# Two relative attentions: the embedded values of eight score tiles, and a batch's values and folds, in every fourth step of the loop

## The chip, the core and the metric

The kernel runs on one core of a Trainium2 chip. The metric is device time in microseconds (us) of one execution of the whole program; three runs of the kernel before gave a median of 2755.65 us. The core's engines work in parallel, each through its own list of instructions in order, and meet only at semaphores: TensorE (PE; its weight loads are shown apart as PEld), VectorE (DVE), ScalarE (ACT), GpSimd (POOL), and SyncE (SP), which issues transfers here.

## What is computed

The network is a chain of residual stages on four lanes (the batch entries `c`) of 512 tokens and 128 channels. Two of its stages are attentions with relative positions, 16 heads of 8 channels. The change touches these two alone. Cut to what matters, the first is

```python
rk, rv = embk[rel], embv[rel]                       # rel = max(t - s, 0)
att = einsum('bhtd,bhsd->bhts', q, k) * scale + einsum('bhtd,tsd->bhts', q, rk)
att = softmax(where(causal, att, -inf))
y = einsum('bhts,bhsd->bhtd', att, v) + einsum('bhts,tsd->bhtd', att, rv)
```

and the second is the same with no causal mask, a distance clipped on both sides, and biases. Each output row is a sum over the keys of the values `v` (called values below) and of the embedded distances `rv` (called embedded values), both weighed by the softmax.

## The kernel before

The program is one list of stages; a `core` stage holds the loop of a relative attention. `which` is 0 for the first attention and 1 for the second. A score tile `t` is 8 queries x 16 heads = 128 rows against all keys in reach; there are 256 of them per attention (`TILES`), `t.G` is their number, and 16 tiles make a batch (`BATCH`), so there are 16 batches. With `which` 0 a batch reaches 1, 2, 3 or 4 blocks of 128 keys (`t.nk`), by turns; with `which` 1 always 4.

The loop is the same on every engine: `core_steps` yields `T_` = 0, 2, 4, ..., and each piece of work is done for the tiles that lag behind `T_` by a constant. One step treats two tiles. On PE a step is:

- `scores` of tiles `T_`-6 and `T_`-5 into banks 0 and 1, each after the exponential of the tile two before has freed the bank (`r_exp`); its last two matmuls (the near positions) also wait for `r_diagonal`;
- `spread` in every second step (`T_` % 4 == 0): the queries of four tiles repeated into bank 6, from which DVE makes the operand `B4` (`diagonal`);
- `turn`: the weights of tiles `T_`-8 and `T_`-7 transposed into banks 2 and 3;
- `inverse` once in a batch;
- in every second step (`T_` % `QUAD` == 0, the step that has a `spread`) what I call a **burst**: `embedded` of four tiles (narrow matmuls of 32 output columns into bank 4 or 5), and in two of a batch's four bursts four of the eight parts of `values` and one `fold` (two matmul groups, also 32 columns wide, into bank 7, or bank 6 with `which` 1). `values` of a batch needs all 16 tiles turned and copied; `fold` needs the embedded values of eight tiles, picked out by DVE's `chosen`.

A step with neither spread nor burst is called plain, and two steps, a plain one and one with a spread, make a pair; a batch has four pairs.

ACT does, in a step, `exps` of two tiles (L1400, each with a read of its sum) and `turned`, the copies of two turned tiles (L1307) into `PT`. `PT` has three slots of eight tiles, so the first copy of every second slot waits for `r_values`, the end of the values of the batch that used the slot before. DVE does, in a step and in this order, `chosen` (L1749, one of four tiles), `position_copy` (L1783 and L1788, only `which` 1, after a fold), `head_copy` (L1809 and L1810, after a batch's values), `inverse` (L1735 and L1737), `maxima` of two tiles (L1765) and `diagonal` (L1758). POOL spreads the queries (L1960, L1970) some steps ahead.

The constants are lags: `EMBED` for `embedded`, `CHOSEN` for `chosen`, `FOLDS` for the two folds of a batch (one pair per attention), `VALUES` for the first part of `values`, `INVERSE`, and `VALUES + QG` for `head_copy`.

## Time and profile before

| | |
|---|---|
| median of three runs | 2755.65 us (2753.82, 2755.65, 2778.35) |
| the profiled execution: its time, its span | 2761.87 us, 2759.9 us |
| PE busy | 2608.3 us (95%) |
| ACT busy | 1839.9 us (67%) |
| DVE busy | 1640.8 us (59%) |
| POOL busy | 1028.1 us (37%) |
| first loop (`which` 0) | from about 612 us to about 1000 us |
| second loop (`which` 1) | from about 1130 us to about 1672 us |

In the timeline a row is a run of like instructions: start, length, engine, line, operation, output<-inputs, shape, count, and in brackets what ended an idle time before it. Every matmul of PE stands on helper lines (L807, L1052), so the work is told by its operands: `table_keys,halves` begins `scores`, `halves,exact` is `spread`, L1052 with `const,low` or `const,slot` is `turn`, `low,table_low` (or `low,shifted`) with 32 columns is `embedded`, `low` alone with 32 columns is `values`, and `slot,const` with 32 columns is `fold`. One matmul of a narrow group is two records. Since matmuls are pipelined, a piece of work is best measured from its first start to the first start of what follows it.

### The profile page before, as it was taken

How to read it: one execution, taken by the hardware profiler on the slowest of the kernel's cores; microseconds unless marked ns; L12 is line 12 of the kernel's file. 1: busy time of each engine (PE TensorE's matmuls, PEld its weight loads, DVE VectorE, ACT ScalarE, POOL GpSimd, SP SyncE). 2: the span in 40 equal slices, each digit the busy share in tenths (PEclk: the TensorE clock that was granted, in tenths of full speed). 3: DMA queues.
4: the chain of work that ended last, by engine and by line, in shares of the span. 5: the costliest groups of instructions: out<-in, count | busy, mean ns of one | idle time of the engine just before them, and what ended most of it. 6: DMA issues, size and time to landing. Idle time of an engine off the chain costs nothing.

```text
span 2759.9 us, 61490 instructions
## 1 busy us (share of the span) xinstructions
PE 2608.3 (95%) x23878; PEld 1795.5 (65%) x23878; DVE 1640.8 (59%) x4295; ACT 1839.9 (67%) x4424; POOL 1028.1 (37%) x876
## 2 busy tenths in 40 slices
PE   7999999999999999999999998998998998988998
PEld 4655656559889884688888884554455664553554
DVE  6564747475455447656665666774774336755774
ACT  6676767526676671778787876875886417766775
POOL 2323324213333320545454543552553015543551
PEclk9999999999999999999999999999999999999999
DMA  1010000000000001000000003210210002101110
GB/s 59 1 44 1 14 4 7 4 9 2 3 2 2 2 2 57 25 2 2 2 2 2 2 2 126 49 36 20 62 44 8 24 14 68 47 20 37 48 39 16
DMA packets 35411, 63.13 MB, mean 23 GB/s; under 512 B 11542, under 2 KB 15670, under 8 KB 34102
## 3 DMA queue, kind: packets, MB, share of 16 engines
q1 hardware_dynamic: 35126, 59.21, 7.8%
q8 instruction: 194, 3.18, 0.5%
q14 instruction: 91, 0.75, 0.1%
HBM read 23.62 MB, written 1.15 MB: 9 GB/s over the span
## 4 chain that ended last, share of the span: by engine, by line
PE 76%; DVE 8%; ACT 8%; issue 3%; SPq 3%; POOL 1%; DMA 1%; DVEq 0%; POOLq 0%; ACTq 0%
PE bank L807 65%; PE bank L1052 6%; PE bank L1189 3%; SPq L772 3%; ACT work L1339 1%; ACT work L1446 1%; PE bank L893 1%; ACT squared L1317 1%; ACT bank L1315 1%; DVE work L1635 1%; ACT squared L1311 1%; DMA work<-work 1%; DVE centered L1566 1%; POOL work L2009 1%; ACT work L1307 1%
## 5 line engine op out<-in xcount | busy, mean ns | idle before, releaser
L1765 DVE TENSOR_REDUCE low<-bank 128x1 f32<-128x512 f32 (+22 forms) x512 | 292.9, 573 | 294.5 <-PE bank L807 292.9
L1307 ACT ACTIVATE low<-bank 128x512 f32<-128x512 f32 (+3 forms) x544 | 434.4, 920 | 0.9 <-PE bank L1052 0.9
L807 PE MATMUL bank<-table_keys,halves 128*128 128x512 f32 (+3 forms) x1536 | 416.5, 379 | 2.6 <-ACT low L1400 2.5
L807 PEld LDWEIGHTS bank<-work 128*64 128x64 f32 (+4 forms) x4192 | 248.4, 144 | 203.0 <-issue 150.1
L807 PE MATMUL bank<-work 128*64 128x128 f32 (+6 forms) x4192 | 343.1, 294 | 38.9 <-DVE work L1859 20.4
L1400 ACT ACTIVATE low<-bank,low 128x512 f32<-128x512 f32 (+23 forms) x384 | 225.0, 586 | 231.3 <-DVE low L1765 226.0
L1960 POOL TENSOR_TENSOR halves<-squared,const 128x512 fp32r<-128x512 f32 x128 | 135.7, 1060 | 507.3 <-PE bank L807 507.3
L1307 ACT ACTIVATE work<-bank 128x512 f32<-128x512 f32 (+4 forms) x389 | 199.2, 538 | 130.5 <-PE bank L807 68.3
L807 PEld LDWEIGHTS bank<-table_keys,halves 128*128 128x128 f32 x1536 | 243.5, 190 | 42.2 <-issue 11.9
L1446 ACT ACTIVATE work<-work 128x192 f32<-128x192 f32 (+1 forms) x512 | 218.7, 431 | 38.4 <-DVE work L1852 38.4
L2009 POOL TENSOR_TENSOR work<-work 128x768 f32<-128x768 f32 x128 | 187.7, 1467 | 138.4 <-DVE work L1863 138.4
L2014 POOL TENSOR_TENSOR work<-work 128x512 f32<-128x512 f32 x128 | 163.4, 1277 | 173.6 <-DMA work<-work 154.2
L807 PE MATMUL bank<-normed,slot 128*128 128x512 f32 x440 | 200.0, 597 | 6.1 <-ACT work L1358 2.4
L807 PEld LDWEIGHTS bank<-halves 128*128 128x128 f32 x1024 | 183.7, 190 | 29.1 <-DVE halves L1758 1.2
L807 PE MATMUL bank<-halves 128*128 128x128 f32 (+27 forms) x1024 | 201.9, 279 | 0.6 <-DVE halves L1758 0.5
L1311 ACT ACTIVATE squared<-centered 128x512 f32<-128x512 f32 x80 | 50.0, 629 | 223.3 <-DVE centered L1566 223.0
L807 PE MATMUL bank<-work,slot 128*128 128x512 f32 (+1 forms) x408 | 192.3, 608 | 5.6 <-ACT work L1307 5.6
L1052 PE MATMUL bank<-const,low 128*128 128x128 f32 x1248 | 182.0, 275 | 2.3 <-ACT low L1307 2.1
L1920 POOL TENSOR_SCALAR normed<-normed,slot 128x512 f32<-128x512 f32 x48 | 75.4, 1571 | 285.8 <-DVE normed L1573 285.5
L807 PE MATMUL bank<-centered,const 128*128 128x512 f32 x256 | 145.4, 650 | 27.9 <-ACT centered L1423 27.9
L2003 POOL TENSOR_TENSOR work<-work 128x512 f32<-128x512 f32 (+1 forms) x64 | 107.5, 1680 | 147.9 <-DVE work L1649 146.7
L1052 PEld LDWEIGHTS bank<-const,low 128*128 128x128 f32 x1248 | 145.0, 141 | 23.1 <-issue 3.2
(203 smaller groups left out, 5385.9 us busy)
## 6 DMA issues: line engine op xcount, KB each, us to landing
work<-work SPq DMA_DIRECT2D x512, 64.0 KB, 2.0
slot<-in_wW SPq DMA_DIRECT2D x4, 1605.5 KB, 6.6
slot<-in_wA SPq DMA_DIRECT2D x4, 837.0 KB, 6.0
table_low<-embv_padded SPq DMA_DIRECT2D x2, 1536.0 KB, 6.3
table<-in_dft SPq DMA_DIRECT2D x1, 3072.0 KB, 11.7
slot<-in_wE SPq DMA_DIRECT2D x2, 584.0 KB, 3.7
squared<-in_x SPq DMA_DIRECT2D x4, 256.0 KB, 5.9
shifted<-embv_padded SPq DMA_DIRECT2D x2, 512.0 KB, 8.3
```

The source lines that it names most:

```text
L772: sp.dma_start(R2[to:to + step, s.n % 3, :], RS[a:a + step, s.n % 3, :]).then_inc(sem(f"w_swapped{s.n % 3}"), 16)
L807: return pe.matmul(o, l, r, start=start, stop=stop)
L1052: last = pe.transpose(o[:, b * P:(b + 1) * P], PR[t.G % 4][:, b * P:(b + 1) * P], ident)
L1189: last = pe.transpose(o[:, (2 * a + blk) * P:(2 * a + blk + 1) * P], PW[:, s.n % 3, 2 * u + a, blk * P:(blk + 1) * P], ident)
L1307: return act.activation(dst, src, ACT.Identity)
L1400: act.activation(PR[t.G % 4][:, 0:n], bank[t.G % 2][:, 0:n], ACT.Exp, bias=NBR[:, t.G % 4:t.G % 4 + 1], accum_out=RSR[:, t.batch % 2, t.g: ...
L1446: last = act.activation(row, row, ACT.Exp, scale=-1.0, bias=small[:, one:one + 1], accum_out=small[:, 4 + one:5 + one])
L1765: dve.tensor_reduce(out=NBR[:, t.G % 4:t.G % 4 + 1], in_=bank[t.G % 2][:, 0:score_columns(t)], axis=AX.X, op=ALU.max, negate=True).then_in ...
L1960: pool.tensor_tensor(A4[:, half, Q % 2, :].rearrange("p (t h) -> p t h", h=HEADS_R), bc(one_lane.unsqueeze(2), [P, 4 * QG, HEADS_R]), bc(k ...
L2003: pool.tensor_tensor(row, row, bc(small_a[:, 8 + s.i % 4, 0:LOC].unsqueeze(2), [P, LOC, 256 - lo]), ALU.mult)\
L2009: pool.tensor_tensor(row, row, bc(small_w[:, s.n % 4, 8:12].unsqueeze(2), [P, 4, 192]), ALU.mult).then_inc(sem("w_weighed"), 1)
L2014: pool.tensor_tensor(R1[:, s.n % 3, :], R1[:, s.n % 3, :], R2[:, s.n % 3, :], ALU.add).then_inc(sem("w_added"), 1)
```

## The change

`embedded` is done for eight tiles at a time, in every fourth step (`T_` % 8 == 0) instead of for four in every second step. All eight parts of a batch's `values` are done in one burst, eight steps of `T_` later than they began before, with the folds after the first part. With `which` 0 both folds of a batch go there; with `which` 1 the first fold goes to the other burst of the batch and the second here. `chosen` and `head_copy` lag accordingly, and the loop has one more step at its end. So a batch has two bursts instead of four, a small one (eight embedded tiles, with `which` 1 one fold) and a big one (eight embedded tiles, the folds, all values). The number of matmuls, activations and vector instructions of the loops stays.

```diff
-SCORES, TURN, EMBED, CHOSEN, QUAD = 6, 8, 12, 14, 4
-FOLDS, VALUES, INVERSE = ((24, 28), (24, 28)), 24, 22
-STEPS = TILES + BATCH + 2
+SCORES, TURN, EMBED, CHOSEN, QUAD, BURST = 6, 8, 16, 18, 4, 8
+FOLDS, VALUES, INVERSE, HEADS = ((32, 32), (24, 32)), 32, 22, 34
+STEPS = TILES + BATCH + 4
...
-                    if T_ % QUAD == 0:
-                        for j in range(QUAD):
+                    if T_ % BURST == 0:
+                        for j in range(BURST):
                             st(embedded, EMBED - j)
                         values(T_)
-                        values(T_ + 1)
                         fold(T_)
-                        values(T_ + 2)
-                        values(T_ + 3)
+                        for j in range(1, BURST):
+                            values(T_ + j)
...
-                        dve.wait_ge(sem("r_head_copied"), BATCHES + sum(VALUES + QG + BATCH * one < T_ for one in range(BATCHES)))
+                        dve.wait_ge(sem("r_head_copied"), BATCHES + sum(HEADS + BATCH * one < T_ for one in range(BATCHES)))
...
-                    k = batch_after(T_, VALUES + QG)
+                    k = batch_after(T_, HEADS)
```

The first place is PE in the second loop, near its end. Before, two bursts of one batch, each between the transposes of a step and the scores of the next (in the order a narrow matmul counts once, so `x16` is four tiles):

```order
L1052 MATMUL bank<-const,low 128x128 x8
L807 MATMUL bank<-low,table_low 32x16x4 x16
L807 MATMUL bank<-low 32x128 x16
L807 MATMUL bank<-slot,const 32x64 x16
L807 MATMUL bank<-low 32x128 x16
L807 MATMUL bank<-table_keys,halves 128x512 x3
L807 MATMUL bank<-halves 128x192 x2
```

Now the big burst at the same place of a batch:

```order
L1052 MATMUL bank<-const,low 128x128 x8
L807 MATMUL bank<-low,table_low 32x16x4 x32
L807 MATMUL bank<-low 32x128 x8
L807 MATMUL bank<-slot,const 32x64 x16
L807 MATMUL bank<-low 32x128 x56
L807 MATMUL bank<-table_keys,halves 128x512 x3
L807 MATMUL bank<-halves 128x160 x2
```

The embedded matmuls are doubled, and 64 values matmuls stand in one place where 32 stood in each of two.

The second place is DVE in the second loop, over the part of a batch in which its position copies (L1783 and L1788 before, one line up in the changed kernel) and head copies (L1809, L1810) stand. Before:

```order
L1749 TENSOR_TENSOR slot<-bank,const 128x4x16x8
L1783 TENSOR_TENSOR low<-bank,low 32x64 x4
L1788 SCALAR_TENSOR_TENSOR centered<-low,centered 32x4x64
L1765 TENSOR_REDUCE low<-bank 128x1 x4
L1758 TENSOR_TENSOR halves<-bank,const 128x512
L1749 TENSOR_TENSOR slot<-bank,const 128x4x16x8
L1783 TENSOR_TENSOR low<-bank,low 32x64 x4
L1788 SCALAR_TENSOR_TENSOR centered<-low,centered 32x4x64
L1765 TENSOR_REDUCE low<-bank 128x1 x2
L1809 TENSOR_TENSOR low<-bank,low 128x64
L1810 TENSOR_TENSOR centered<-centered,low 128x64
```

Now, after the small burst and then after the big one:

```order
L1748 TENSOR_TENSOR slot<-bank,const 128x4x16x8
L1782 TENSOR_TENSOR low<-bank,low 32x64 x4
L1787 SCALAR_TENSOR_TENSOR centered<-low,centered 32x4x64
L1764 TENSOR_REDUCE low<-bank 128x1 x4
L1757 TENSOR_TENSOR halves<-bank,const 128x512
L1748 TENSOR_TENSOR slot<-bank,const 128x4x16x8
L1764 TENSOR_REDUCE low<-bank 128x1 x4
L1757 TENSOR_TENSOR halves<-bank,const 128x512
L1748 TENSOR_TENSOR slot<-bank,const 128x4x16x8
L1782 TENSOR_TENSOR low<-bank,low 32x64 x4
L1787 SCALAR_TENSOR_TENSOR centered<-low,centered 32x4x64
L1808 TENSOR_TENSOR low<-bank,low 128x64
```

The second position copy has moved one pair later and the head copies have come to stand right behind it, ahead of the maxima; `chosen` stands where it stood, but two of a batch's four no longer have a burst just ahead of them.

## Rows read from the trace of the kernel before

**Rows 1.** Busy time by engine, 100 us of the second loop (stretch, length, engines, clock).
```profile
1340.00:1440.00 100.00, 99.83 (x1498) 86.42 (x1498) 61.39 (x117) 81.51 (x150) 52.71 (x52) 1.00 0.01 2
```

**Rows 2.** PE's waits, second loop, 1240 to 1640 us (us in total, times, longest).
```profile
PE bank L807 <- ACT low L1400: 0.5, 3, 0.2
```

**Rows 3.** PE's timeline in the second loop: two pairs, with bursts.
```profile
1385.45 1.07 PE L1052 MATMUL bank<-const,low 128*128 128x128 f32 x8
1386.45 0.65 PE L807 MATMUL bank<-low,table_low 128*32 128x64 f32 x32
1387.04 0.96 PE L807 MATMUL bank<-table_keys,halves 128*128 128x512 f32 x3
...
1393.84 0.96 PE L807 MATMUL bank<-table_keys,halves 128*128 128x512 f32 x3
...
1400.35 0.65 PE L807 MATMUL bank<-low,table_low 128*32 128x64 f32 x32
1400.82 1.06 PE L807 MATMUL bank<-low 128*32 128x128 f32 x32
1401.69 0.63 PE L807 MATMUL bank<-slot,const 128*32 128x64 f32 x32
1402.14 1.06 PE L807 MATMUL bank<-low 128*32 128x128 f32 x32
1403.13 0.96 PE L807 MATMUL bank<-table_keys,halves 128*128 128x512 f32 x3
```

**Rows 4.** PE's timeline where the second loop starts: a pair without burst.
```profile
1133.73 0.97 PE L807 MATMUL bank<-table_keys,halves 128*128 128x512 f32 x3 [0.67 <-ACT low L1400]
...
1136.15 1.03 PE L1052 MATMUL bank<-const,low 128*128 128x128 f32 x8
1136.94 0.94 PE L807 MATMUL bank<-table_keys,halves 128*128 128x512 f32 x3
...
1139.85 0.96 PE L807 MATMUL bank<-table_keys,halves 128*128 128x512 f32 x3
```

**Rows 5.** ACT's timeline in the second loop: one step and the next exponentials.
```profile
1406.64 2.01 ACT L1307 ACTIVATE low<-bank 128x512 f32<-128x512 f32 x2
1408.44 0.64 ACT L1400 ACTIVATE low<-bank,low 128x512 f32<-128x512 f32 x1
...
1409.07 0.68 ACT L1400 ACTIVATE slot<-bank,low 128x512 f32<-128x512 f32 x1
...
1409.73 2.10 ACT L1307 ACTIVATE low<-bank 128x512 f32<-128x512 f32 x2
```

**Rows 6.** DVE's timeline in the second loop: a position copy and the next maximum.
```profile
1402.39 0.97 DVE L1783 TENSOR_TENSOR low<-bank,low 32x64 f32<-32x64 f32 x4 [0.63 <-PE bank L807]
1403.40 0.47 DVE L1788 SCALAR_TENSOR_TENSOR centered<-low,centered 32x256 f32<-32x256 f32 x1
1404.38 0.69 DVE L1765 TENSOR_REDUCE low<-bank 128x1 f32<-128x512 f32 x1 [0.51 <-PE bank L807]
```

**Rows 7.** PE's timeline in the first loop, one block of keys: scores, spread, turn.
```profile
736.97 0.51 PE L807 MATMUL bank<-table_keys,halves 128*128 128x128 f32 x3
...
737.65 0.67 PE L807 MATMUL bank<-halves,exact 128*128 128x512 f32 x2
738.16 0.38 PE L1052 MATMUL bank<-const,low 128*128 128x128 f32 x2
```

**Rows 8.** DVE's timeline in the same stretch: a maximum and the diagonal.
```profile
737.17 0.28 DVE L1765 TENSOR_REDUCE low<-bank 128x1 f32<-128x120 f32 x1 [0.77 <-PE bank L807]
...
738.36 0.69 DVE L1758 TENSOR_TENSOR halves<-bank,const 128x512 fp32r<-128x512 f32 x1 [0.22 <-PE bank L807]
```

**Rows 9.** DVE's timeline in the first loop: chosen, inverse, next maxima.
```profile
716.17 0.69 DVE L1749 TENSOR_TENSOR slot<-bank,const 128x512 f32<-128x512 f32 x1 [0.71 <-PE bank L807]
716.78 0.24 DVE L1735 RECIPROCAL low<-low 128x16 f32<-128x16 f32 x1
...
717.26 0.66 DVE L1765 TENSOR_REDUCE low<-bank 128x1 f32<-128x128 f32 x2
```

## Prediction

> **What bounds the kernel now.** I read the busy time by stretch first. In the second loop PE is busy 99.83 of 100 us at a granted clock of 1.00, which is its 2.4 GHz level, ACT 81.51 and DVE 61.39 [rows 1]. So time moves there only if PE's stream gets shorter or PE begins to wait. The view of waits says that PE waits for ACT only 0.5 us in 400 [rows 2]. That is not the whole story, because a matmul record lasts until its modelled end and hides a short wait; so I measured from first start to first start in PE's timeline. A pair of steps with a burst of embedded values alone takes 1393.84 - 1387.04 = 6.80 us; the next pair, whose burst also holds values and a fold, takes 1403.13 - 1393.84 = 9.29 us, the once-a-batch inverse included [rows 3].
>
> The row that decides the case stands at the start of the second loop, where nothing is embedded yet: a pair without a burst. It takes 1139.85 - 1133.73 = 6.12 us [rows 4]. So a burst's removal can be read directly, with what PE then waits for.
>
> **What a burst costs beyond its matmuls.** After eight transposes the first narrow matmul starts 1386.45 - 1385.45 = 1.00 us after the first transpose [rows 3]; where scores follow instead, they start 1136.94 - 1136.15 = 0.79 us after it [rows 4]. So entering costs 0.21. Four embedded tiles take 1387.04 - 1386.45 = 0.59 if scores follow, and 1400.82 - 1400.35 = 0.47 if values follow [rows 3]; so leaving costs 0.12. The Trainium skill's page "TensorEngine Tiling (Array Packing)", Tiling Modes, Key Properties, says that changing the tiling mode drains TensorE; the trace agrees with these 0.21 and 0.12, and by that rule alone each burst taken away is worth their sum.
>
> Two bursts of four go in every batch, 64 in both loops. By pure PE time that is 64 x 0.33 = 21 us. By whole pairs it is less: 6.80 less its 0.47 of embedded work is 6.33, against the 6.12 measured without a burst, so 0.21 per burst and 0.42 per batch. The difference of 0.12 is a wait that shows up when the burst no longer covers it: ACT and DVE use a burst to catch up.
>
> **Second loop, part by part, for a batch without its inverse** (which is the same in both). From the same rows, two parts of values take 1401.69 - 1400.82 = 0.87, a fold 1402.14 - 1401.69 = 0.45 [rows 3].
>
> Before: two pairs of 6.80 and two with 6.80 + 2 x 0.87 + 0.45 = 8.99, sum 31.58. After: two pairs without burst, 2 x 6.12; the small burst's pair 6.80 + 0.47 + 0.45 = 7.72; the big burst's pair 6.80 + 0.47 + 0.45 + 4 x 0.87 = 11.20; sum 31.16. That is -0.42 per batch. Three things are given back.
>
> (a) The position copy. It starts 0.25 after its fold ends (1402.39 against 1402.14) and DVE is free after 0.97 + 0.04 + 0.47, at about 1403.9, or 1.8 after the fold's end [rows 3, 6]. Today two parts of values follow the fold, and the next maximum starts 1404.38 - 1403.13 = 1.25 after its scores do, held by PE and not by the copy. After the small burst no values follow: scores start 0.12 after the fold, so the maximum could start at 1.37. It starts at 1.8, so about 0.45 late, and behind the maximum stand the exponential and, through `r_exp`, the scores of two tiles later. A plain step has no slack there. I charge it in full: +0.45 per batch. The lower bound is nothing, if the next step's spread absorbs it. After the big burst the copy lies under 3.0 us of values and costs nothing; if that cover were gone it would cost the same 0.45.
>
> (b) ACT's pace. In a step ACT needs 0.63 and 0.66 for two exponentials and 1.80 for two copies, 3.09 [rows 5], so 6.18 per pair, against 6.12 for a pair without burst. It has no idle time left in these pairs: +0.06 for each of two, +0.12 per batch. Behind the big burst the two copies that wait for `r_values` start only at its end. They take 1.80 from 0.2 after it, so until 2.0; the first exponential of the next step needs its maximum, which starts at 1.3 and takes 0.69, so it is ready at 2.0 as well. I charge nothing for it, and it is the tightest place of the change.
>
> (c) The end of the loop. The last fold now needs a `chosen` that stands behind a position copy in DVE's queue: from the end of the last embedded tiles 0.45 (fold) + 0.25 + 1.5 (copy) + 0.7 (chosen) = 2.9, where PE gets there after 0.45 + 0.43 = 0.9; it waits about 2.0, and of that 0.7 comes back, since the copy that ended the loop before is out of the way. +1.3 once.
>
> Sum of the second loop: 16 x (-0.42 + 0.45 + 0.12) + 1.3 = +3.7 us.
>
> **First loop.** The gain is the same 0.42 per batch at most. ACT has room there, having one to four blocks to treat. But DVE's queue is tight where scores are short. With one block of keys the spread starts at 737.65, the transposes at 738.16, and DVE's diagonal at 738.36 [rows 7, 8]. Without a burst the next scores start some 0.2 after the transposes do (an estimate: 0.79 is for eight), and a tile's take 737.65 - 736.97 = 0.68, so they end at 739.04 and their maximum could start 0.20 later, as 737.17 follows 736.97: at 739.24. DVE now goes from the diagonal straight to `chosen` (0.61, as the diagonal too has) and reaches the maximum at 738.36 + 0.61 + 0.61 = 739.58, 0.34 late. In the step that also has the inverse (717.26 - 716.78 = 0.48 [rows 9]) it is 0.82 late. Each further block of keys gives PE about 0.3 more (from 0.2 and 0.68 here to 0.79 and, as 1.25 less the 0.20, 1.05 with four), while DVE's queue stays: 0.04 and 0.52 with two blocks, 0 and 0.22 with three, 0 with four. Sum 1.94 over four batches, 0.49 per batch, charged in full, since the scores of these steps wait for their exponential. 16 x (-0.42 + 0.49) = +1.1 us.
>
> Together +4.8, against the profiled execution's 2761.87 us: 2766.7. That execution lies 6.2 above the median of the runs; on the median's scale it is 2755.65 + 4.8 = **2760.5 us**. What a measurement can tell from no change is about 1%, 27.6 us; every term here is below it.
>
> **Rivals.**
>
> *The gain lands whole.* If the 0.12 that ACT and DVE take back were an effect of the loop's start and (a), (b) and the first loop's queue were absorbed, it is 64 x 0.33 = 21 us faster: 2734.5. With half of the losses it is about 2748. For it: the skill's drain rule above, and PE's 99.83%. Against: the pair without burst is already 0.12 per burst slower than its matmuls. Chance of the part under 2750: 0.20.
>
> *Slower, by ACT's blocked copies.* The copies of two tiles stand in ACT's queue ahead of the next two exponentials and wait for the end of the big burst. The Trainium skill's page "TensorE: Matmul & The Clock Gate", Part 1, Engine queue depths, says that ScalarE's queue is strictly first in, first out; no run here shows an exception. By that rule nothing of the exponentials could pass, and if they had been ready all along the copies would cost their whole 1.80. The point at which it decides is 2.0 us behind the burst, where copies and maximum meet. Every 0.1 by which the copies are later costs 32 x 0.1 = 3.2 us; wholly exposed it is 16 x 1.80 in the second loop, and about two thirds of that in the first with its shorter copies: 48 us, 2804. Against the whole price: the maxima cannot be ready before the scores that follow the burst. Chance of over 2783: 0.08; of a part of it, 2768 to 2783, 0.17.
>
> *PE's clock falls.* The big burst is 0.94 + 0.45 + 3.48, nearly 5 us of narrow matmuls, where 2.78 stood (1403.13 - 1400.35) [rows 3] at full clock [rows 1]. If half of each in the second loop went at 1.2 GHz, 16 x 2.5 = 40 us: 2800. Against it: the narrow matmuls follow each other without a gap. Chance 0.03.
>
> *No effect beyond noise, as forecast*, 2750 to 2768: the remaining 0.52. Under 2728 there is no case, only the unknown; I leave it 0.03, taken from the first rival's share.
>
> **How the numbers follow.** The range reaches from 2735, where the whole gain stands, to 2781, where half of the blocked copies' price does; about 0.1 is left out above and little below. Faster by over 1%: 0.03. Slower by over 1%: 0.08 + 0.03 = 0.11, of which I give 0.10, since the lower ends of these cases stay inside. Within 1%: 0.87.
>
> **What would show it.** In the changed kernel's timeline: pairs without burst of about 6.2 us in the second loop; a big burst's pair of 11.2 and a small one's of 7.7, followed by a plain step 0.45 longer than the others, with the position copy ahead of its maximum. In the views of waits and of DVE: in the first loop with one block of keys, maxima that start right behind `chosen` with no idle time before them. ACT's idle time falls together into one place per batch, the big burst. The forecast is wrong if pairs without burst take 6.3 or more (then ACT is the bound, and it is slower), if they take under 6.05 (then it is faster), or if the clock of a stretch of 100 us falls under 1.00.

## The result, and the profile after

| | before | after |
|---|---|---|
| median | 2760.07 us (8 runs, 2753.82 to 2778.35) | 2785.22 us (8 runs, 2782.39 to 2786.23) |
| ratio after / before | | 1.0083 (95% interval 1.0068 to 1.0097) |
| the profiled execution: time, span | 2761.87, 2759.9 us | 2785.75, 2783.8 us |
| first loop, first spread to last narrow matmul | 424.8 us | 438.5 us |
| second loop, the same | 540.8 us | 556.2 us |

The change makes the kernel 25 us (0.8%) slower. The two loops lose 13.7 and 15.4 us; the stretch between them takes 93.3 us in both profiles. The stages behind the second loop take 1084.0 us where they took 1088.9; in the profiles of the experiments below the same stages take 1082.8 to 1103.1, so that difference is not put down to the change. Everything that is to be explained is in the loops. (The first loop of the kernel before ends at 1036.9 us, not at about 1000.)

The view of windows, second loop (columns as in [rows 1]):

```profile
1340.00:1440.00 100.00, 97.10 (x1502) 84.28 (x1503) 60.20 (x110) 74.96 (x143) 47.20 (x44) 1.00 0.01 2
```

PE was busy 99.83 of 100 us [rows 1] and now is 97.10, at the same granted clock of 1.00. PE has begun to wait. The view of waits of PE (us in total, times, longest), over both loops, of the kernel before (612 to 1671 us):

```profile
PE bank L1052 <- ACT low L1307: 2.7, 5, 0.9
PE bank L807 <- ACT low L1400: 2.5, 10, 0.7
PE bank L807 <- issue: 1.0, 3, 0.4
...
PE bank L807 <- DVE halves L1758: 0.5, 1, 0.5
```

and of the changed kernel (612 to 1700 us), where L1399, L1306 and L1757 are the same lines:

```profile
PE bank L807 <- issue: 11.3, 19, 1.2
PE bank L807 <- ACT low L1399: 6.1, 17, 0.7
PE bank L1052 <- ACT low L1306: 5.3, 13, 1.5
...
PE bank L807 <- DVE halves L1757: 2.2, 8, 0.5
PE bank L807 <- POOL halves L1959: 2.1, 3, 0.7
PE bank L807 <- DVE slot L1748: 1.8, 1, 1.8
```

The new first row is "issue": time in which PE waited for nothing that the profile shows. The prediction had no term for it. PE's timeline shows where it lies. This is a big burst of the second loop, the counterpart of the last lines of [rows 3]:

```profile
1400.15 1.04 PE L1052 MATMUL bank<-const,low 128*128 128x128 f32 x8
1401.12 1.10 PE L807 MATMUL bank<-low,table_low 128*32 128x64 f32 x64
1402.03 0.62 PE L807 MATMUL bank<-low 128*32 128x128 f32 x16
1402.47 0.63 PE L807 MATMUL bank<-slot,const 128*32 128x64 f32 x32
1402.92 0.61 PE L807 MATMUL bank<-low 128*32 128x128 f32 x12
1404.01 3.03 PE L807 MATMUL bank<-low 128*32 128x128 f32 x100 [0.49 <-issue]
1406.98 0.96 PE L807 MATMUL bank<-table_keys,halves 128*128 128x512 f32 x3
```

Embedded values (1402.03 - 1401.12 = 0.91), a part of values (0.44) and the fold (0.45) take what their rows of before said. Then the seven parts of values that are left stop after 12 records and go on at 1404.01, with no operand to wait for: all of them were there. By starts the pause is 0.76 us; the row shows less of it, since a record lasts until its modelled end. The view of transfers, 40 slices of 0.425 us from 1395 to 1412 us, shows what else happened:

```profile
GB/s 0 19 0 0 0 0 0 0 0 0 0 0 0 0 0 39 0 0 0 0 0 0 0 39 0 0 0 0 0 0 0 19 0 0 0 0 39 0 0 0
...
q8 instruction: 3, 0.05, 1.2%
q14 instruction: 2, 0.02, 0.4%
```

The three tall slices are transfers of 16,384 bytes on the queue of kind "instruction", q8; the first begins at 1401.50, and PE goes on 2.5 us later.

I counted these pauses over both loops, as starts of two narrow matmuls inside a run that lie more than 0.13 us apart, less the usual 0.05: 9 pauses with 3.45 us before, 33 with 19.58 us after. Of these, 3 before (1.15 us) and 4 after (2.37 us) lie at the loops' ends, where an operand is waited for. The others, 6 with 2.30 us before and 29 with 17.21 us after, end 2.2 to 2.9 us after a q8 transfer began. That makes +14.9 us, about half of the 29 us that the two loops lose. The counts of the experiments below are those of all such pauses.

### The profile page after: what moved, and what is told of

It reads as the page before. It is cut to its first block, busy times and chain, and to the rows that moved or that the text cites. A ratio compares the mean times of both kernels' runs of the same rounds, so it can differ in the third digit from the quotient of the medians.

```text
span 2783.8 us, 61475 instructions
## 1 busy us (share of the span) xinstructions
PE 2609.7 (94%) x23878; PEld 1801.3 (65%) x23878; DVE 1640.8 (59%) x4295; ACT 1827.6 (66%) x4424; POOL 1027.2 (37%) x876
## 3 DMA queue, kind: packets, MB, share of 16 engines
HBM read 23.62 MB, written 1.15 MB: 9 GB/s over the span
## 4 chain that ended last, share of the span: by engine, by line
PE 71%; DVE 10%; ACT 10%; issue 3%; SPq 2%; POOL 2%; DMA 1%; DVEq 0%; POOLq 0%; ACTq 0%
PE bank L807 61%; PE bank L1052 5%; PE bank L1188 3%; SPq L772 2%; ACT low L1306 1%; ACT work L1338 1%; ACT low L1399 1%; PE bank L893 1%; ACT work L1445 1%; ACT squared L1316 1%; ACT bank L1314 1%; DVE low L1764 1%; DVE work L1634 1%; DMA work<-work 1%; ACT squared L1310 1%
## 5 line engine op out<-in xcount | busy, mean ns | idle before, releaser
L1306 ACT ACTIVATE low<-bank 128x512 f32<-128x512 f32 (+3 forms) x544 | 432.0, 912 | 161.5 <-PE bank L807 157.7
L1399 ACT ACTIVATE low<-bank,low 128x512 f32<-128x512 f32 (+23 forms) x384 | 224.2, 586 | 107.7 <-DVE low L1764 104.7
L1306 ACT ACTIVATE work<-bank 128x512 f32<-128x512 f32 (+4 forms) x389 | 199.1, 538 | 130.3 <-PE bank L807 67.3
```

Source lines behind the costliest of these rows:

```text
L1306: return act.activation(dst, src, ACT.Identity)
L1399: act.activation(PR[t.G % 4][:, 0:n], bank[t.G % 2][:, 0:n], ACT.Exp, bias=NBR[:, t.G % 4:t.G % 4 + 1], accum_out=RSR[:, t.batch % 2, t.g: ...
```

## The steps, one by one

The median time from a step's first scores to the next step's, by `T_` modulo 16, second loop, batches of the first block (us). The middle line is worked out from before by the prediction's own prices: 0.47 for four embedded tiles, 0.435 for a part of values, 0.45 for a fold and for the exposed copy, 0.21 for a burst taken away.

| step | 6 (inverse) | 8 | 10 | 12 | 14 | 0 | 2 | 4 | sum |
|---|---|---|---|---|---|---|---|---|---|
| before | 3.15 | 6.15 | 2.81 | 6.19 | 2.83 | 3.99 | 2.78 | 4.06 | 31.96 |
| by the prices | 3.15 | 4.88 | 3.26 | 3.32 | 2.83 | 8.39 | 2.78 | 3.38 | 31.99 |
| after | 3.65 | 4.85 | 3.46 | 3.20 | 3.05 | 9.05 | 2.83 | 3.31 | 33.40 |

Step 0 holds the big burst and is 0.66 too long. Step 10 has the exposed position copy: +0.65 here, and +0.48 on the mean over the four blocks, where 0.45 was forecast. Step 2, behind the big burst, is 0.05 longer than before: ScalarE's blocked copies cost next to nothing. Steps 6 and 14 are longer by 0.50 and 0.22, on the mean over the blocks by 0.23 and 0.13: ScalarE's pace, where 0.12 together was charged (in step 6 the second tile's transposes, which need ScalarE's work, start 2.67 behind the first scores where they started 2.34 behind).

In the first loop step 0 is too long by 0.6 on the mean, and the steps behind a pair without burst grow where scores are short, from 2.43, 1.66, 2.30 and 1.91 to 3.15, 2.13, 2.82 and 2.15 (steps 6 and 14 with one and with two blocks of keys); step 4 with one block takes 2.99 where its parts give about 2.1.

## The experiments

The theory is now: **TensorE runs out of instructions in a long run of narrow matmuls**, because they use up instructions faster than these are fetched. The rivals are that the pauses belong to the narrow matmuls themselves or to the loop around them (banks, copies), that ScalarE's blocked copies are what costs, and, for the first loop, several candidates for the wait behind a pair without burst.

### The runs of narrow matmuls alone

```diff
+                if s.which:
+                    for wide in (P, 64):
+                        for n in range(256):
+                            strip = 32 * (n % 4)
+                            pe.matmul(bank[7][strip:strip + 32, 0:wide], k_("fold")[:, 32 * (n // 4 % 4):32 * (n // 4 % 4) + 32],
                                      const[:, 0:wide], start=True, stop=True)
+                        for _ in range(6):
+                            pe.matmul(bank[7][:, :], k_("mean"), const[:, 0:T], start=True, stop=True)
```

> The kernel before with useless work ahead of its second loop, to measure the disputed thing alone: 256 matmuls into 32 columns with 128 moving columns (as the values), six wide matmuls of 512, 256 matmuls into 32 columns with 64 moving columns (as the embedded values), six wide ones; no engine but TensorE has anything to do with them. By the rows of the loops the first run lasts 256 x 0.054 = 13.9 us with 73 records of TensorE and its weight loads in a us, the second 256 x 0.029 = 7.5 us with 136. In the changed kernel every pause ended 2.2 to 2.9 us after a fetch of instructions began and 110 to 240 records behind it. Theory (instruction supply): the 64-column run, which uses 150 to 210 records in 1.1 to 1.5 us, pauses at about every 256th record for about 1 us, 3 or 4 times, and lasts 10.5 to 12 us; the 128-column run uses them in 2.1 to 2.9 us and pauses little, under 0.6 at a time, 14 to 15.5 us; every pause ends 2.2 to 2.9 us after a fetch began. Rival (the pauses come from the loop: the other engines' use of the banks, the copies that read them): no pause in either run, 13.9 and 7.5 us.

PE's timeline in that stretch:

```profile
1126.60 14.18 PE L1005 MATMUL bank<-const 128*32 128x128 f32 x512
1140.71 5.42 PE L1008 MATMUL bank<-const 128*128 128x512 f32 x12
1146.06 2.66 PE L1005 MATMUL bank<-const 128*32 128x64 f32 x175
1149.85 1.99 PE L1005 MATMUL bank<-const 128*32 128x64 f32 x128 [1.14 <-issue]
1153.32 1.99 PE L1005 MATMUL bank<-const 128*32 128x64 f32 x128 [1.48 <-issue]
1157.07 1.36 PE L1005 MATMUL bank<-const 128*32 128x64 f32 x81 [1.75 <-issue]
1158.36 5.42 PE L1008 MATMUL bank<-const 128*128 128x512 f32 x12
```

and the transfers of the same place, slices of 0.4 us from 1145 to 1161 us:

```profile
GB/s 0 0 0 0 0 0 41 0 0 0 0 0 0 0 0 41 0 0 0 0 0 0 0 41 0 0 0 0 0 0 0 0 41 0 0 0 0 0 0 0
...
q8 instruction: 4, 0.07, 1.6%
```

This settles it. The run of 128 columns goes through without a pause; the run of 64 columns, alone on the chip's core, stops after every 128 matmul records, with which go as many weight loads: 256 instructions, and one transfer of 16,384 bytes for each such portion. It lasts 1158.36 - 1146.06 = 12.3 us where its matmuls alone take 7.5 by the prices of the loops, a little more than expected. Every pause ends 2.3 to 2.7 us after a transfer began. Portions start 1153.32 - 1149.85 = 3.47 and 1157.07 - 1153.32 = 3.75 us apart, so 256 instructions in about 3.5 us is what arrives when they are used at once: some 70 a us. Values use 73 a us and just get by; embedded values and folds use 136 and more, and eat up what was fetched ahead. The Trainium skill's page "Runtime: NRT & Kernel Launch", section "Instruction fetch mechanics", says that instructions come in blocks of 16 KiB, 256 of them, which the portions of 128 and 128 records agree with; it also says that the fetch is hidden because dispatch is slower, and there the measurement decides: for this run it is not hidden, and 1.1 to 1.8 us of waiting stand ahead of each of the last three portions.

### The values in two portions, the embedded values in eights

```diff
-FOLDS, VALUES, INVERSE, HEADS = ((32, 32), (24, 32)), 32, 22, 34
+FOLDS, VALUES, INVERSE, HEADS = ((24, 32), (24, 32)), 24, 22, 34
...
+                        first = T_ - 4 if T_ % BATCH == 0 else T_
-                        values(T_)
+                        values(first)
                         fold(T_)
-                        for j in range(1, BURST):
-                            values(T_ + j)
+                        for j in range(1, QUAD):
+                            values(first + j)
```

> The changed kernel with one part undone: the eight embedded tiles stay in every fourth step, but a batch's values are again done in two portions of four parts, one in each of its two bursts, each behind a fold or with one in it. The number of bursts, of narrow matmuls and of instructions is that of the changed kernel; only the longest run of narrow matmuls falls from about 5 us to 0.94 + 0.45 + 1.74 = 3.1 us. Theory (TensorE runs out of instructions in a long run of narrow matmuls): the pauses inside the runs fall from 33 with 19.6 us in sum to about the 9 with 3.5 us of the kernel before, and the position copy of each fold lies under three parts of values again (1.3 us), so the second loop loses the 16 us of pauses and the 16 x 0.45 of the copy: 2755 to 2766, a ratio of 1.000 to 1.002 against the kernel before. Rival 1 (a pause belongs to the narrow matmuls or to the embedded values of eight tiles, wherever they stand): the pauses stay and only the copy is hidden, about 2778, 1.005. Rival 2 (ScalarE's copies that wait for the end of the values are what costs): that end stays in the same step, so the time stays within 5 us of 2785, 1.007 to 1.009.

Measured: 2771.88 us against 2764.43, 1.0043 (1.0021 to 1.0065). Its first profile was taken at a mean clock of 0.943, so a second one was wanted:

> The same kernel as the one with the values split over the two bursts, for a second profile, since the first was profiled at a mean granted clock of 0.943. Theory (instruction supply): pauses as in the first profile, 20 to 28 with 8 to 12 us in sum, since they hang on the fetches and not on the clock; a span near 2768. Rival (the pauses there came from the lower clock): fewer than 15.

Pauses: 24 with 10.4 us in the first profile, 27 with 11.6 in the second (mean clock 0.984). So they do not hang on the clock, and with the shorter run their time falls to a little over half but does not go: a run of 3.1 us is still too long, and the theory's 9 pauses and 1.000 to 1.002 were missed. The end of the values stays in the same step and half of the loss is gone, so ScalarE's blocked copies are not the cause. The changed kernel's ACT timeline behind a big burst says the same:

```profile
1407.15 2.01 ACT L1306 ACTIVATE low<-bank 128x512 f32<-128x512 f32 x2 [5.70 <-PE bank L807]
1408.96 0.65 ACT L1399 ACTIVATE low<-bank,low 128x512 f32<-128x512 f32 x1
```

The copies start right behind the burst and the exponential 1408.96 - 1406.98 = 2.0 us after the scores do, as forecast.

The position copy is settled by the same pair of kernels. DVE's timeline of the changed kernel behind a small burst, whose next scores start at 1388.30:

```profile
1388.45 0.97 DVE L1782 TENSOR_TENSOR low<-bank,low 32x64 f32<-32x64 f32 x4 [0.68 <-PE bank L807]
1389.46 0.47 DVE L1787 SCALAR_TENSOR_TENSOR centered<-low,centered 32x256 f32<-32x256 f32 x1
1389.97 1.29 DVE L1764 TENSOR_REDUCE low<-bank 128x1 f32<-128x512 f32 x2
```

and of the second profile with the values split, scores at 1382.36:

```profile
1381.20 0.97 DVE L1783 TENSOR_TENSOR low<-bank,low 32x64 f32<-32x64 f32 x4 [1.12 <-PE bank L807]
1382.21 0.47 DVE L1788 SCALAR_TENSOR_TENSOR centered<-low,centered 32x256 f32<-32x256 f32 x1
1383.64 0.69 DVE L1765 TENSOR_REDUCE low<-bank 128x1 f32<-128x512 f32 x1 [0.96 <-PE bank L807]
```

There the maximum starts 1.67 us after the scores, straight behind the copy, and two maxima run together; here it starts 1.28 after them and VectorE has been idle for 0.96. Step 10 goes from 3.46 back to 2.81.

### All values at once, the embedded values in fours

```diff
-FOLDS, VALUES, INVERSE = ((24, 28), (24, 28)), 24, 22
+FOLDS, VALUES, INVERSE = ((28, 28), (24, 28)), 28, 22
...
-                        values(T_)
-                        values(T_ + 1)
+                        at_once = QG if T_ % BATCH == 12 else 0
+                        for j in range(0, min(1, at_once)):
+                            values(T_ + j)
                         fold(T_)
-                        values(T_ + 2)
-                        values(T_ + 3)
+                        for j in range(1, at_once):
+                            values(T_ + j)
```

> The kernel before with one part of the change alone: four bursts in a batch with four embedded tiles each, as before, but all eight parts of a batch's values in one of them (the fourth), so that a run of narrow matmuls lasts up to 0.47 + 0.45 + 8 x 0.435 = 4.4 us. In the second loop the first fold then has no values behind it, and its position copy costs 16 x 0.45 = 7 us by the prediction's own term; nothing else of the change is in it. Theory (instruction supply): pauses inside the long runs, at least 20 in both loops and 5 to 15 us in sum, though nothing is embedded in eights: 2772 to 2782, 1.004 to 1.008. Rival (the pauses belong to the embedded values of eight tiles or to the new places of the bursts): no more pauses than the 9 of the kernel before, and only the copy's price: 2765 to 2769, 1.002 to 1.003.

Measured: 2776.44 us, 1.0040 (1.0025 to 1.0056), 15 pauses with 7.0 us, of which 12 with 4.8 us end behind a q8 transfer as above. More pauses than before (6 of that kind) although nothing is embedded in eights, so the eights are not needed for them; but fewer than the 20 expected. That only four embedded tiles, not eight, go ahead of the values may be why; no run shows it apart. The larger part of this kernel's loss is the position copy: the plain step behind the small burst is 1.10, 1.04, 0.56 and 0.65 longer in the four blocks, 0.84 on the mean, 13 us in all, where I had put 7.

### Wide matmuls in the middle of the big burst

```diff
                         for j in range(1, BURST):
+                            if j == 3 and 0 <= T_ - VALUES < TILES and (T_ - VALUES) % BATCH == 0:
+                                for _ in range(8):
+                                    pe.matmul(bank[7][:, 384:512], k_("mean"), const[:, 0:P], start=False, stop=False)
                             values(T_ + j)
```

> The changed kernel with eight extra matmuls of 128 columns, of no use, after the third part of the values in each of the 32 big bursts. By the rows they cost 0.8 us (a transpose of 128 columns takes 0.1) and 0.33 for leaving and entering the narrow form, 1.13 x 32 = 36 us, but only 16 instructions. Theory (instruction supply): while they run, instructions arrive faster than they are used, the pauses fall from 19.6 us to under 8, and the kernel becomes only 18 to 26 us slower than the changed one: 2803 to 2811, 1.015 to 1.018 against the kernel before. Rival (a pause has to do with the narrow matmuls themselves, their banks or what other engines do): all pauses stay and the price is whole: 2818 to 2825, 1.021 to 1.023.

Measured: 2835.49 us, 1.0266 (1.0250 to 1.0283), slower than both expectations. PE's timeline shows why:

```profile
1435.80 0.95 PE L807 MATMUL bank<-low 128*32 128x128 f32 x28
1436.68 2.05 PE L1149 MATMUL bank<-const 128*128 128x128 f32 x16
1438.66 2.39 PE L807 MATMUL bank<-low 128*32 128x128 f32 x80
```

The eight matmuls take 1438.66 - 1436.68 = 1.98 us and not 1.13: I had priced them by a transpose of the same size, which is one record of 0.11 us, and a float32 matmul is two such records, 0.22 us; the rest is the change of form. With this price the added work is 32 x 1.98 = 63 us. The kernel is 1.0266 - 1.0083 = 1.83% of the time before slower than the changed one, 50.6 us; so some 13 us came back, with several us of uncertainty. By the same count as above the pauses fell from 19.58 to 8.10 us (13 of them, 2.15 us of it the wait for `chosen` at the second loop's end), 11.5 less. Price and pauses together give 52. That is the theory's mechanism, with a price that was wrong; the 2803 to 2811 expected of the whole were missed for it.

### What holds the first loop

The prediction's term for the first loop was that `chosen` and the inverse hold up the maxima in VectorE's queue. Moving `chosen` tests it:

```diff
-                    st(chosen, CHOSEN)
                     position_copy(T_)
...
                     st(diagonal, SCORES - 2)
+                    st(chosen, CHOSEN)
```

> The changed kernel with one line of VectorE moved: chosen stands at the end of a step's list, behind the maxima and the diagonal, instead of at its head. It tests the prediction's term for the first loop, that where scores are short VectorE's chosen and inverse hold up the maxima and so TensorE: 0.49 per batch. Theory (that term is right): the steps with and after the inverse in the batches of one and two blocks of keys, now 3.15, 2.13, 2.82 and 2.15 us, go back to about the 2.4, 1.7, 2.3 and 1.9 of the kernel before, and the time falls by about 16 x 0.49 = 8 us: a ratio of 1.0055 against the kernel before. Rival (those steps are held by something else, ScalarE's copies or GpSimd): no step gets shorter, 1.0083.

Measured: 1.0091 (1.0074 to 1.0108), steps of 3.17, 2.13, 2.65 and 2.15. Only the third step moved, by 0.17: the term's mechanism falls. PE's timeline in this kernel shows what holds step 14 with one block instead:

```profile
723.87 0.38 PE L1052 MATMUL bank<-const,low 128*128 128x128 f32 x2
724.00 0.53 PE L807 MATMUL bank<-table_keys,halves 128*128 128x128 f32 x3
724.81 0.44 PE L807 MATMUL bank<-halves 128*128 128x128 f32 x2 [0.28 <-DVE halves L1757]
```

The near scores wait for the diagonal itself. It is made from the spread, which stands just ahead in the step; the burst of embedded values behind every spread used to cover it. In the kernel before they follow 0.39 behind the first three matmuls here, and 0.81 in this kernel as in the changed one; with two blocks 0.81 and 0.59 in steps 6 and 14, where they followed 0.45 and 0.46 behind.

The largest of the four, step 6 with one block, is another case that I had overlooked. The timeline of the kernel before, and then of the changed one, all engines:

```profile
715.68 1.99 ACT L1307 ACTIVATE low<-bank 128x512 f32<-128x512 f32 x2
716.03 0.55 PE L807 MATMUL bank<-table_keys,halves 128*128 128x128 f32 x3
...
717.42 0.62 PE L1052 MATMUL bank<-const,low 128*128 128x128 f32 x4
...
717.88 0.60 PE L1052 MATMUL bank<-const,slot 128*128 128x128 f32 x4
```

```profile
718.82 0.53 PE L807 MATMUL bank<-table_keys,halves 128*128 128x128 f32 x3
...
719.18 0.39 PE L807 MATMUL bank<-halves 128*128 128x128 f32 x2
719.25 1.98 ACT L1306 ACTIVATE low<-bank 128x512 f32<-128x512 f32 x2
...
720.49 0.63 PE L1052 MATMUL bank<-const,low 128*128 128x128 f32 x4
...
721.37 0.63 PE L1052 MATMUL bank<-const,slot 128*128 128x128 f32 x4 [0.26 <-ACT low L1306]
```

There the near scores follow 0.36 behind (719.18 - 718.82) and wait for nothing. ScalarE's copies of the two tiles ahead, which still have four blocks of keys, start 0.43 behind the step's first scores where they started 0.35 ahead of them, and the second transposes, which wait for these copies, start 0.88 behind the first instead of 0.46.

I took all four steps for the diagonal's. So I put the spread, and the diagonal on VectorE, at the head of the step:

```diff
+                    st(spread, SCORES - 2)
                     st(scores, SCORES)
                     st(scores, SCORES - 1)
-                    st(spread, SCORES - 2)
...
+                    st(diagonal, SCORES - 2)
                     st(chosen, CHOSEN)
...
-                    st(diagonal, SCORES - 2)
```

> The changed kernel with the spread at the head of a step on TensorE, ahead of the two tiles' scores, and the diagonal made from it at the head of VectorE's list. It tests what holds up the steps behind a pair without burst in the first loop, now that moving chosen did nothing. Theory (the near scores of the next step wait for the diagonal itself, which starts only after the spread and used to be covered by the burst): the diagonal gets ready a step's scores earlier, the steps of 3.15, 2.13, 2.82 and 2.15 us in batches of one and two blocks go back to within 0.15 of 2.4, 1.7, 2.3 and 1.9, the waits of TensorE for the diagonal vanish, and the time falls by 16 x 0.5 = 8 us: a ratio near 1.0055. The pauses in the narrow runs stay as they are, near 33. Rival (ScalarE's copies or the inverse hold those steps): no step gets shorter, 1.008 to 1.009; or the earlier spread waits for GpSimd, and it is slower, over 1.010.

Measured: 2796.58 us, 1.0126 (1.0102 to 1.0150): slower, as the second rival had it. The four steps take 4.03, 2.71, 3.63 and 2.50 us, of which about 0.5 is the next spread, now ahead of the scores. PE's timeline at the same place of a batch, and its waits from 620 to 1040 us:

```profile
732.36 0.55 PE L807 MATMUL bank<-table_keys,halves 128*128 128x128 f32 x3
732.75 0.39 PE L807 MATMUL bank<-halves 128*128 128x128 f32 x2
...
734.50 0.73 PE L807 MATMUL bank<-halves,exact 128*128 128x512 f32 x2 [0.33 <-POOL halves L1959]
```

```profile
PE bank L807 <- POOL halves L1959: 8.1, 8, 2.2
PE bank L807 <- issue: 5.9, 8, 1.1
```

The near scores now follow 0.39 behind the first three matmuls (732.75 - 732.36) where they followed 0.81 behind (724.81 - 724.00). So in this step the diagonal was the wait. In step 6 with one block the second transposes still start 0.88 behind the first: there it was not. And the gain is handed on: the next spread comes earlier and waits for GpSimd's copies of the queries, 8.1 us in all.

GpSimd had cost a little already (the row of 2.1 us, three times, above): its line that spreads a lane's values waits for the end of the big burst and holds up the queries behind it.

```diff
-                    lane, rest = divmod(T_ - (BATCH + 2), NT * BATCH)
+                    lane, rest = divmod(T_ - (BATCH + 4), NT * BATCH)
```

> The changed kernel with one line of GpSimd moved: the spreading of a lane's values, which waits for the end of the values of the lane before, is put one step later in GpSimd's list, behind the spread of the queries that the next scores need. Theory (in the three steps of the first loop where that wait now lasts until the big burst's end, the late spread holds TensorE up by 0.9 us each): 2.6 us faster than the changed kernel, about 2782 to 2784, and the steps that follow the big burst at a change of lane get 0.9 us shorter. Rival (the wait costs nothing): no difference from the changed kernel, 1.0083, and those steps stay at about 3.0 us. The difference is near what can be measured; the steps' lengths decide.

The step in question goes from 2.99 to 2.06 and the row vanishes from PE's waits, so the mechanism stands. The time does not show it: 1.0096 (1.0081 to 1.0110), with 36 pauses and 20.1 us in this profile. A term of 2.6 us is below what these runs resolve.

### Versions made from the findings

Three bursts in a batch, none over about 2.3 us:

```diff
-FOLDS, VALUES, INVERSE, HEADS = ((32, 32), (24, 32)), 32, 22, 34
+FOLDS, VALUES, INVERSE, HEADS = ((28, 32), (28, 32)), 24, 22, 34
...
+                    parts = {8: (0, 1, 2), 12: (-1, 0, 1), 0: (-2, -1)}.get(T_ % BATCH, ())
...
```

> A version made from the findings: three bursts in a batch of which none is longer than about 2.3 us by its parts: eight embedded tiles and three parts of the values (2.24), a fold and three parts (1.75), eight embedded tiles, a fold and two parts (2.26); each fold has values behind it, chosen stands last in VectorE's list, and GpSimd's lane values one step later. Theory (instruction supply and the three confirmed terms): one burst less than before in each of 32 batches saves 32 x 0.21 = 6.7 us, no run is long enough for many pauses (under 12, under 5 us in sum), nothing is given back: 2 to 9 us faster than the kernel before, a ratio of 0.997 to 0.999. Rival (a burst of eight embedded tiles itself brings the pauses): 20 or more pauses and 1.002 to 1.006.

Measured: 2770.21 us, 1.0024 (1.0009 to 1.0040), 9 pauses with 5.1 us. The number of pauses is as the theory wants, with embedded values in eights (their sum just over the 5 us expected); the gain of the missing burst is not there. In the first loop's batches of one block the pair without burst takes 2.06 + 3.17 = 5.23 us, where it took 2.81 + 2.43 = 5.24 with one, although its four embedded tiles have moved elsewhere. The near scores of its step 6 do not wait (they follow 0.37 behind); the second transposes wait for ScalarE's copies as above. I took it for the diagonal then. Next came the same version with the spread and the diagonal first (and `chosen` back at its place), and the same move in the kernel before, as a control:

> The version with three bursts in a batch (measured at 1.0024), chosen back at its old place, with the spread and the diagonal at the head of a step. Theory (the diagonal is what its one pair without burst lost): the inverse's step, 0.3 to 0.7 us longer there than in the kernel before in three of four batches of both loops, gives that back, 5 to 8 us: 0.9995 to 1.0010. Rival (another wait holds that step): 1.002 or more.

> The kernel before with only the spread and the diagonal moved to the head of a step, as a control for the two others. Theory (before, every spread had a burst behind it that covered the diagonal): nothing to win, 0.998 to 1.001. Rival (the diagonal held the kernel before too): 0.996 or less; or the earlier spread waits for GpSimd: over 1.002.

Measured: 1.0002 (0.9987 to 1.0017) for three bursts and **0.9954 (0.9936 to 0.9971)** for the control, 2751.09 us against 2765.12. The first has the number that was expected but not for the reason given: its pair without burst gets longer in batches of one block (1.64 + 4.04 = 5.68), and with two and three blocks only 0.12 and 0.28 shorter. The control, for which I expected nothing, beats both kernels with all four bursts kept; it has 6 pauses with 2.4 us. Part of the difference between the two profiles lies in the first 16 tiles of the first loop, 17.6 us against 22.6, where the clock was 1.00 in the control from the start and lower before (below); the other tiles give 5.8 us in the first loop and the whole second loop 2.8, spread over the steps. The rival put down for such a number, that the diagonal held the kernel before too, does not fit: there the near scores already follow 0.39 behind with one block and 0.45 with two, as in the control. Which wait it is was not taken apart and stays open. With the spread first in both, the version with three bursts is about 13 us slower than the kernel with four. Not all of that need be the burst, since the version also splits the values in three and moves the folds and GpSimd's line; its PE waits 8.6 us, 28 times, for ScalarE's copies, where the control's waits 3.1 us, 7 times.

## Why the prediction was off

It forecast 2760.5 us, no change that a measurement can tell, within 2735 to 2781; the median is 2785.2, 4 us above the range and still within 1%.

- **The step that failed** is the big burst's pair, "6.80 + 0.47 + 0.45 + 4 x 0.87 = 11.20": a run of narrow matmuls was priced as the sum of shorter ones. The sum had no term for TensorE's instructions, as if they were always there. In a run twice as long they run out, for about 0.5 us a big burst (17.21 us over 32 of them, some in small ones): 14.9 us more than before, about half of what the loops lose, and more than the whole gain of 2 x 16 x 0.42 = 13.4. The kernel before had the sign of it, 6 such pauses, but I read the short runs as free of them.
- **The clock.** The prediction looked in those runs for a falling clock and found the wrong resource: in the window shown the granted clock is 1.00 while PE pauses.
- **The gain per burst** is right: the steps that lost a burst, 4 and 12, are 0.07 and 0.12 shorter than the prices give. So is the pair without burst: steps 2 and 4 take 2.83 + 3.31 = 6.14, where 6.12 was read and about 6.2 forecast.
- **(a) The position copy**, 0.45 a batch, came out at 0.48, with the maxima straight behind it as described, and went away when values covered it.
- **(b) ScalarE** was forecast at 0.12 a batch in the second loop and is nearer 0.36; the rival of its blocked copies, 0.05 at step 2, falls.
- **(c) The loop's end** was to wait about 2.0 us for `chosen`; the row `DVE slot L1748` has 1.8, once.
- **The first loop's 0.49 per batch** was right in place and size (0.55 by the steps) and wrong in mechanism: not `chosen` ahead of the maxima. Of the 2.25 us by which the steps of four batches grow, 1.23 stands in three steps whose near scores wait for the diagonal behind the spread, and 0.72 in one whose transposes wait for ScalarE's copies, which the prediction had given room in this loop; 0.30, step 6 with three blocks, was not taken apart. Right by luck, then: a fix aimed at the mechanism named did next to nothing, and one aimed at the diagonal alone could not mend the largest step.
- **GpSimd's wait for `r_values`** was overlooked. I followed that semaphore to ScalarE and not to its second reader: three steps of 0.9 us, 2.6 us.
- In the first loop's first 18 us the granted clock was 0.72 in the profile of before and 0.60 in that of after, and 1.00 in those of most variants, among them the one that differs by GpSimd's line alone. So some 2 us of the profiles' difference there are probably not the change's doing.
- Added up by the profiles, the forecast +4.8, the pauses' 14.9, 0.24 x 16 = 3.8 of ScalarE's pace, GpSimd's 2.6 and the 2 us of clock make 28.1 of the 29.1 us that the loops lose.

## What to carry to other kernels

Price a run of small matmuls by its instructions as well as by its matmuls: what was measured in a short run holds only while the instructions fetched ahead last, and a pause put down to "issue" in the middle of a run whose operands are all there is the sign. Work that looks like mere overhead between two dependent steps may be their cover, so before it is merged away, list every reader of what stands ahead of it, on every engine. And test a term that came out right too: its number can be met by another wait.

## What the runs showed of the hardware

- In a long run of 32-column matmuls of 64 moving columns, TensorE got 256 instructions in about 3.5 us; a pause ended 2.2 to 2.9 us after a 16,384-byte transfer on the instruction queue began. A run that used 73 instructions a us went on for 14.18 us without a pause.
- Eight wide matmuls (16 matmul records in 1.98 us) in the middle of each of 32 long runs of narrow ones took the pauses from 19.58 to 8.10 us.
- A float32 matmul of 128 columns took 0.22 us on the full array (two records 0.11 apart), a transpose of the same size 0.11 (one record).
